# Projections of batches 1 to 3 in pieces beside the attention heads, in an unrolled program

## The reference

```python
Q, K, V = (proj(Wq, bq), proj(Wk, bk), proj(Wv, bv))     # 16 heads of 8 columns
S = jnp.einsum('bhnd,bhmd->bhnm', Q, K) / dh ** 0.5
W_tau = jax.nn.softmax(S, axis=-1)
W_sigma = 1.0 / ((1.0 + jnp.abs(S) / b_) ** 2 + t_ ** 2)
W_sigma = W_sigma / W_sigma.sum(axis=-1, keepdims=True)
f = 0.5 * tau + 0.5 * sigma        # tau = W_tau @ V, sigma = W_sigma @ V
y = f @ Wo.T + bo                  # then a layer norm with ln_w, ln_b, and x is added
```

## Time and profile before

| | us |
|---|---|
| median of 3 runs (2052.15 to 2053.83) | 2053.55 |
| the profiled execution | 2050.47 |
| its span, first to last instruction | 2048.6 |
| first instruction of the heads on VectorE | 97.43 |
| last instruction of the heads | 1611.70 |
| `mix_experts` to the end | the rest |

### The profile page before, as it was taken

How to read it: one execution, slowest core, us unless ns; L and a number is a source line. 1 busy time by engine, 2 the same in 40 slices (tenths; PEclk the granted TensorE clock), 3 DMA queues, 4 the chain that set the end, 5 groups by cost and what they waited for, 6 DMA issues and landing times. The chain is left out here.

```text
span 2048.6 us, 33898 instructions
## 1 busy us (share of the span) xinstructions
PE 1571.4 (77%) x8452; PEld 572.2 (28%) x8579; DVE 1800.0 (88%) x3699; ACT 1634.4 (80%) x1459; POOL 1419.3 (69%) x1070
## 2 busy tenths in 40 slices
PE   4477777877777777777777778777777587788866
PEld 2212222222222222222222222222221243366655
DVE  5799999999999999999999999999998288755556
ACT  3279999999999999999999999999999311222243
POOL 1398999889998899988999899998998112000010
PEclk9689999999999999999999999999999788877878
DMA  3300000000000000000000000000000000000001
GB/s 106 110 4 15 12 12 12 15 14 12 12 12 15 14 12 12 12 15 14 12 12 13 16 12 12 12 13 16 12 12 6 1 1 0 1 0 0 0 1 41
DMA packets 28862, 31.74 MB, mean 15 GB/s; under 512 B 5209, under 2 KB 16544, under 8 KB 28832
## 3 DMA queue, kind: packets, MB, share of 16 engines
q1 hardware_dynamic: 28832, 31.40, 5.0%
HBM read 22.74 MB, written 8.39 MB: 15 GB/s over the span
## 5 line engine op out<-in xcount | busy, mean ns | idle before, releaser
L860 POOL TENSOR_TENSOR sigma_weights<-grown 128x1024 f32<-128x1024 f32 x448 | 845.7, 1894 | 0.0
L718 DVE TENSOR_SCALAR sigma_weights<-ps_sig 128x512 int32<-128x512 int32 x1024 | 693.2, 677 | 26.5 <-PE ps_sig L617 26.5
L604 PE MATMUL ps_acc<-tau_weights,v_operand 128*9 128x512 f32 x2048 | 529.5, 596 | 134.3 <-ACT sigma_weights L779 134.0
L725 DVE TENSOR_TENSOR running_max<-ps_sig,running_max 128x512 f32<-128x512 f32 x896 | 608.2, 679 | 0.0
L833 POOL TENSOR_SCALAR grown<-sigma_weights,shape_operand 128x1024 f32<-128x1024 f32 x448 | 501.7, 1120 | 139.9 <-DVE sigma_weights L718 139.9
L617 PE MATMUL ps_sig<-q_operand,k_operand 96*128 96x512 bf16 x1024 | 400.2, 391 | 180.3 <-DVE running_max L725 165.2
L604 PE MATMUL ps_acc<-sigma_weights,v_operand 128*9 128x512 f32 x2048 | 531.4, 597 | 0.1
L766 ACT ACTIVATE sigma_weights<-sigma_weights,shape_operand 128x2048 f32<-128x2048 f32 x256 | 508.6, 1987 | 11.2 <-POOL sigma_weights L860 11.2
L807 ACT ACTIVATE tau_weights<-ps_tau 128x1024 f32<-128x1024 f32 x512 | 510.8, 998 | 8.0 <-PE ps_tau L635 8.0
L779 ACT ACTIVATE sigma_weights<-sigma_weights 128x2048 f32<-128x2048 f32 x256 | 484.6, 1893 | 0.0
L635 PE MATMUL ps_tau<-q_operand,k_operand 128*128 128x512 bf16 x897 | 277.8, 379 | 7.9 <-DMA q_operand<-max_rows 0.4
(11 more groups left out here) (172 smaller groups left out, 1511.5 us busy)
## 6 DMA issues: line engine op xcount, KB each, us to landing
q_operand<-q_parts SPq DMA_DIRECT2D x192, 48.0 KB
k_operand<-k_parts SPq DMA_DIRECT2D x64, 144.0 KB
q_parts<-parts SPq DMA_DIRECT2D x12, 256.0 KB, 2.9
k_parts<-parts SPq DMA_DIRECT2D x12, 256.0 KB, 2.9
x_res<-in_L_attn_x SPq DMA_DIRECT2D x4, 512.0 KB, 7.0
q_operand<-max_rows SPq DMA_DIRECT2D x128, 2.0 KB
out<-x_res SPq DMA_DIRECT2D x4, 512.0 KB, 3.2
experts<-in_L_ffn_expert_w SPq DMA_DIRECT2D x1, 512.0 KB
```

What stands on the lines that cost most here:

```text
L604: mm = pe.matmul(ps_acc[32 * q:32 * q + COLS, :], vop[:, (slot - 1 + kind) % SLOTS, j, :], weights[:, half * HALF:(half + 1) * HALF], star ...
L718: dve.tensor_scalar(sig[:, tile % SIG_RING, cols].bitcast(I32), ps_sig[:, half, :].bitcast(I32), SIGN_OFF, None, ALU.bitwise_and)\
L725: dve.tensor_tensor(run[:, slot, cols], ps_sig[:, half, :], run[:, slot, cols], ALU.max)\
L860: pool.tensor_tensor(sig[:, tile % SIG_RING, :], t, t, ALU.mult)\
```

## The change

`load_weights`, `project_heads` and `attend_heads` become one block, `attend_heads`, without hardware loops. Its slots are numbered g from 0 to 533 over all heads.

- Before slot 0 only batch 0 is projected. SP loads the x of batches 0 and 1 first; weights and biases are loaded from ScalarE's queue. The x of batches 2 and 3 is loaded after the operands of heads 0 to 2.
- The projections of batches 1, 2 and 3 are pieces, generators that yield the slot at which they are due, from slots 0, 128 and 256 on, each over 21 slots. `Beside.upto` puts a piece between the instructions of its slot. The preparation of the tree's weights and Wo is pieces at slots 24 to 31.
- A batch's q and k are projected in halves of 512 tokens. The two banks `ps_side` are used in turn by all pieces (h0, h1, q0, k0, q1, k1, v0, v1). The buffer `parts` holds one half. ScalarE makes the high part from PSUM and the middle part from `rest`; VectorE makes `rest`; GpSimd makes all low parts. SP stores per half.
- `ps_tau` has one buffer of two banks (its other two became `ps_side`). PE waits with tile g for the exponential of tile g-1.
- Lags: `PV_LAG` 7 to 9, tau 12 to 13. `take_sums` moves with it.
- Both bf16 rows of the row maximum are made by VectorE (ScalarE's L796 is gone).
- GpSimd's copies of v and of the constants are gone: PE and the others read them in place.
- The last step of a head multiplies in PSUM in place and adds from there into `f_tokens`, in the layout that `mix_experts` needs. ScalarE's copy `f_tile` in `mix_experts` (L975) is gone; ln_b is added by GpSimd beside the heads.

The tile that ScalarE squares is the same before and after.

In the diff below, `store_parts` is SP's (due at slots 13 and 19 of a batch's pieces), the first `yield` PE's, the second VectorE's, `high` and `middle` ScalarE's (due at 9, 10, 14.7, 15.5 and at 11, 12, 16.5, 17), the third `yield` GpSimd's.

```diff
-TAU_SHIFT = 4
-PV_LAG = 7
+PV_LAG = 9
+TAU_LAG = 13
+class Beside:
+    def __init__(self, pieces):
+        self.pieces, self.due = pieces, -1.0
+    def upto(self, slot):
+        while self.due <= slot:
+            self.due = next(self.pieces, float("inf"))
...
-        ps_tau = ps("ps_tau", [P, 2, 2, HALF])
+        ps_tau, ps_sig = ps("ps_tau", [P, 2, HALF]), ps("ps_sig", [P, 2, HALF])
+        ps_side = [ps(f"ps_side{i}", [P, HALF]) for i in range(2)]
...
+            def store_parts(b, g):
+                sp.wait_ge(low_ready, 4 * b + 2 * g + 2)
+                for s, scratch in enumerate((q_parts, k_parts)):
+                    for i in range(PARTS):
+                        sp.dma_start(scratch[b * H:(b + 1) * H, i, :, g * HALF:(g + 1) * HALF], parts[:, s, i, :])\
+                            .then_inc(stored, 16)
...
+                for i, (g, s) in enumerate((g, s) for g in range(2) for s in range(2)):
+                    n = u(f"{'qk'[s]}{g}")
+                    yield t0 + 8 + i
+                    read(u(f"h{g}"))
+                    take(n)
+                    done(pe.matmul(bank(n)[:, :], wt[:, s, :], zt[:, g * HALF:(g + 1) * HALF], start=True, stop=True), n)
...
+            def tau_scores(g):
-                        wait(pe, tau_done, g - 1)
+                wait(pe, tau_done, g)
...
+                    yield t0 + (10, 11, 15.5, 16.2)[i]
+                    dve.wait_ge(hi_ready, 4 * b + i + 1)
+                    wait(dve, low_ready, 4 * b + i - 1)
+                    done(dve.scalar_tensor_tensor(out=rest[:, s, :], in0=bank(n)[:, :], scalar=(bq, bk)[s][:, 0:1],
+                                                  in1=parts[:, s, 0, :], op0=ALU.add, op1=ALU.subtract), n)
...
+                def high(i):
+                    g, s = pairs[i]
+                    n = u(f"{'qk'[s]}{g}")
+                    arrived(n)
+                    wait(act, stored, 16 * 2 * PARTS * (2 * b + g))
+                    act.activation(parts[:, s, 0, :], bank(n)[:, :], ACT.Identity, bias=(bq, bk)[s][:, 0:1]).then_inc(hi_ready, 1)
+                def middle(i):
+                    g, s = pairs[i]
+                    read(u(f"{'qk'[s]}{g}"))
+                    act.activation(parts[:, s, 1, :], rest[:, s, :], ACT.Copy).then_inc(mid_ready, 1)
...
+                    yield t0 + (11.5, 12.2, 17, 17.6)[i]
+                    pool.wait_ge(mid_ready, 4 * b + i + 1)
+                    pool.tensor_tensor(parts[:, s, 2, :], rest[:, s, :], parts[:, s, 1, :], ALU.subtract).then_inc(low_ready, 1)
...
+            def complete(of):
+                dve.wait_ge(norm_step, normed(of) + 2)
+                dve.tensor_tensor(result(of - 1), turned[:, :, 0:2, 0:DH], result(of - 1), ALU.add).then_inc(misc_done, 1)
```

More of the change, by code:

```diff
@@ L24 @@
 NH = B * H
+TILES = NH * TB
 HALF = 512
@@ L565, in _, with take, read, done @@
+            beside.upto(ALL)
         @block.tensor
         def _(pe):
-            def turn_running(slot, half, before):
-                wait(pe, misc_done, before)
+            def take(n):
+                wait(pe, side_read[n % 2], n // 2)
+            def read(n):
+                pe.wait_ge(side_read[n % 2], n // 2 + 1)
+            def done(mm, n):
+                mm.then_inc(side_ready[n % 2], 1)
+            def turn_four(n, tile_of):
+                take(n)
+                for t in range(4):
+                    mm = pe.transpose(bank(n)[:, t * P:(t + 1) * P], tile_of(t), ident[:, :])
+                done(mm, n)
@@ new lines, in side, with sigma_scores @@
+            def side():
+                for b in range(B - 1):
+                    yield from project(b + 1, b * BATCH_SLOTS)
+                    if b == 0:
+                        yield from prepare(PREPARE_AT)
+            def sigma_scores(g, half):
+                slot, keys = g // TB % SLOTS, slice(g % TB * P, (g % TB + 1) * P)
+                wait(pe, run_ready, 2 * g - 1 + half)
+                pe.matmul(ps_sig[:, half, :], kop[0:SIGMA_ROWS, slot, keys],
+                          qop[0:SIGMA_ROWS, slot, half * HALF:(half + 1) * HALF], start=True, stop=True).then_inc(sig_ready, 1)
@@ L653, in _ @@
-            stages(pe, stage)
-            turn_sums(NH, misc_before(NH + 1) + 1)
+                        weights = tau[:, (i - TB) % TAU_RING] if kind == 0 else sig[:, i % SIG_RING]
+                        mm = pe.matmul(ps_acc[32 * q:32 * q + COLS, :], v[:, (of - 1 + kind) % (2 * H), j, :],
+                                       weights[:, half * HALF:(half + 1) * HALF], start=j == 0, stop=j == TB - 1)
+                mm.then_inc(pv_done, 1)
+            beside = Beside(side())
+            pe.wait_ge(ident_step, 2)
@@ new lines, in _ @@
+            beside = Beside(side())
+            dve.memset(qop[64:P, :, :], 0.0).then_inc(pads_set, 1)
+            dve.memset(kop[64:P, :, :], 0.0).then_inc(pads_set, 1)
+            dve.wait_ge(pads_set, 2)
+            dve.memset(kop[MROW:MROW + 2, :, :], 1.0).then_inc(pads_set, 1)
+            dve.memset(ps_acc[:, :], 0.0).then_inc(acc_set, 1)
+            pieces = project(0, 0)
+            for _ in range(TB + 1):
+                next(pieces)
+            dve.wait_ge(wt_turned, 1)
+            dve.tensor_copy(wt[:, 0:3, :], ps_tau[:, 0, 0:3 * D].rearrange("p (i d) -> p i d", i=3)).then_inc(wt_ready, 1)
@@ new lines, in normal, with copy_turned @@
+            def normal(z0, b, g):
+                act.wait_ge(shift_ready, z0 + 1)
+                alone(act, act_passed)
+                for t in range(4 * g, 4 * g + 4):
+                    ins = act.activation(h[:, t, :], xt(b, t), ACT.Identity, bias=shift[:, t:t + 1], scale=rstd[:, t:t + 1])
+                ins.then_inc(z_ready, 1)
+            def copy_turned(n, g):
+                arrived(n)
+                done(act.activation(zt[:, g * HALF:(g + 1) * HALF], bank(n)[:, :], ACT.Copy), n)
@@ L1312, in _ @@
         def _(pool):
-            with pool.Fori(0, B) as b:
+            for b in range(B):
                 pool.wait_ge(z_ready, b * TB + TB)
@@ L1320, in _ @@
         def _(pe):
-            with pe.Fori(0, B) as b:
+            for b in range(B):
                 for t in range(TB):
@@ L1550, in _ @@
         def _(sp):
-            with sp.Fori(0, B) as b:
+            for b in range(B):
                 sp.wait_ge(x_done, b * 2 + 2)
```

1116 lines of the change are left out of this document (536 added, 580 removed).

## The result

| us | before | after |
|---|---|---|
| median of 19 runs each | 2051.13 (2049.8 to 2053.83) | 2056.44 (2053.76 to 2062.95) |
| ratio after / before | | 1.0026, 95% interval 1.0019 to 1.0033 |
| the profiled execution | 2050.47 | 2054.09 |
| its span | 2048.6 | 2052.3 |
| first magnitude on VectorE | 97.43 | 45.99 |

The change costs 0.26%, where I had forecast a gain of 0.75%. The time lies in the range of the forecast, on the wrong side of no change. 51 us are won at the start, and all of it, and 4 more, is lost before the span ends. (The forecast started from 2053.55, a median of three runs; over 19 runs the kernel before has 2051.13.)

The account below looks back on a forecast made before the run. ScalarE sets the length of a head (23.2 us), VectorE close behind. The terms -50.4 + 7.0 - 2.7 - 10.1 + 21.9 + 16.8 + 3.2 - 1.1 = -15.4 take 2053.55 to 2038, range 2016 to 2058.

Parts of the forecast that it names:

- The start: Before the heads: VectorE's first magnitude comes at 47 us against 97.4, -50.4, range 42 to 52.
- The ramp: First magnitude to first tau, bound by VectorE: a later tau slot, batch 1's pieces and two waits add +7.0.
- Two are on the path: Beside the pieces: two stalls, the store and the two banks, are on the path, +16.8 together, from 0 to 34.
- Both stops I named: Third high part waits for the store, 4.1 three times; tau waits for two banks, 2.2 for batches 2 and 3.
- The pieces on ScalarE: Behind slot 13: projection pieces and preparation lengthen ScalarE, the bound engine, by +21.9.
- L796: Steady head: this row-maximum instruction leaves ScalarE, 0.16 x 63 = -10.1, if ScalarE stays solid.
- The single `ps_tau` at nothing: In the heads: one tau buffer costs nothing, cover 0.9 us a slot; rival that it bites, 2070, chance 0.14.
- The sign I had promised for "wrong": ScalarE idle before tau in every head, ended by PE: the single buffer, kernel near or above its old time.
- The last step of a head: VectorE's L696 took 1.32 in a head, 0.22 with GpSimd idle; new form priced 0.15, successor near 0.2.
- The middle parts: Beside the heads: casts moved from VectorE to ScalarE put 12 x 0.5 = 6 us on the path.
- The tail and what follows: End of the heads: slower tau tiles and two slots more for PE, +3.2; then `f_tile` leaves the path, -1.1.

Follow-up runs that it names:

- e1: Changed kernel with only the store of the second half moved on SyncE from slot 19 to 22, behind the operand loads: 2045.9, ratio 0.9976.
- e2: Changed kernel with only `parts` holding both halves, so the third high part waits for nothing of its batch: 2034.6, ratio 0.9921.
- e10: e3 with `rest`, middle and low parts of the second half one slot later: 2012.2, ratio 0.9812.
- e5: Changed kernel without the projections of batches 1 to 3 (heads read batch 0's operands and v): 1989.2, ratio 0.9695.
- e7: Changed kernel with the first part of the row maxima (L796) back on ScalarE: 2058.5, ratio 1.0038.
- e6: Kernel before the change with one buffer of tau scores for two, nothing else: 2051.9, ratio 1.0006.
- e9: e3 with `PV_LAG` 8 for 9, the slots of a head's sums and their turning moving too: 2070.7, ratio 1.0094.
- e12: e9 with the turning of a head's sums back in the slot it has with `PV_LAG` 9: 2021.6, ratio 0.9857.
- e8: e3 with the middle-part casts on VectorE right behind `rest`, not on ScalarE: 2026.1, ratio 0.9878.
- e3: Changed kernel with three edits: second-half store behind the operand loads, `parts` for both halves, second-half q and k projections in slots 12 and 13: 2014.3, ratio 0.9825.
- e11: e8 with the middle parts computed on VectorE from PSUM and the high part, not cast from `rest` in SBUF: 2018.6, ratio 0.9842.

## Why the prediction was wrong

The account by stretches of the span, in us. "Last dense tau" is the last tau tile with sigma work beside it (1593.79 + 1.00 before, 1599.48 + 0.92 after, where 0.92 is its pitch; its record of 1.78 ends at 1601.26, and by that end 0.9 moves from the tail to the row above).

| | forecast | measured |
|---|---|---|
| start to the first magnitude | -50.4 | -51.4 |
| ramp, to the first tau | +7.0 | 39.1 - 31.5 = +7.6 |
| first tau to last dense tau | +25.9 | 1515.3 - 1465.9 = +49.4 |
| tail, to the end of the heads | +3.2 | 18.8 - 16.9 = +1.9 |
| what follows | -1.1 | 433.1 - 436.9 = -3.8 |
| sum | -15.4 | +3.7 |

- **The start: right.** 45.99 for 47, but partly by luck. The first half's store had landed at 27.6 for my 29.7, and the second's at 37.6 for 40.4 (landing 1.8 after the last issue, not 2.4); head 0's operand then took 4.7 from its last issue (40.69) to PE's first scores (45.37), where I had 2.4. The two errors nearly cancel. The ramp was right too (7.6 for 7.0).
- **The step that failed: "Two are on the path".** Stops measure 36.6 for 16.8, and this is 19.8 of the 19.1 us that the forecast missed; the others cancel. Both stops I named were there, in the slots named and near their size: 4.9 for 4.1 each, 3.1 for 2.2 each. What was missing:
  - 11.4 us, SyncE's queue. I asked of each queue only whether the moved work fits beside it, not which instruction with a wait stands ahead of which with a due date. The second store waits for GpSimd's low parts; an operand needed three slots later stood behind it. e1 shows it.
  - 4.2 us, VectorE ahead of ScalarE. I let only ScalarE wait for the high part's turn, but `rest` waits for that high part on an engine that is up to a slot ahead, with every magnitude behind it. e2 shows that the store alone doesn't make this stop, e10 that the slot of `rest` does. Its length is about what PE lost at the half clock (2.84 for 1.51 us), a cost that my sum left out; that part is argued, not tested.
- **The pieces on ScalarE: right.** 22.0 by e5 for 20.0 (21.9 less the preparation's 1.9, which e5 keeps).
- **L796: mis-sized.** 0.107 a head for 0.16, and, as it seems, only in undisturbed heads: 4.4 by the spans and 2.0 by the medians, for 10.1. I took a start-to-start distance of one short instruction as its cost; the head's period is the measure. That L796's removal lengthened nothing else stands (e7).
- **The single `ps_tau` at nothing: right** (e6: 0.9 us by the medians, with 0.7 before each of the last tiles; in e10, with the changed order, no stop behind the first tau), but its cover is thin: moving one turn by a slot costs 49 us (e9 against e12). The sign I had promised for "wrong", idle time before tau in every head, is absent in after and present in part in e9.
- **The last step of a head:** 0.212 us in the median, for 0.22.
- **The middle parts.** I priced them as a loss of 6 us against leaving them on VectorE. From first tau to last dense tau, e8 takes 29.8 over e5 and e3 26.1; without their stops of 13.7 and 5.5 that is 16.1 and 20.6, so ten of the casts lie on ScalarE's path with 4.5. But on VectorE they made the kernel 11.8 slower (e8), 4.3 even without waits for GpSimd (e11). In e11 that loss lies before the first tau and behind the heads; beside batches 2 and 3 the two placements came out even (1481.3 and 1481.8). The advice of the Trainium skill that I weighed, Perfetto Trace Analysis, section Optimizing Scalar/DVE Operations, to offload a saturated VectorE to ScalarE, was right here by the times of e3, e8 and e11, but not because ScalarE is free: the gain is the waits for GpSimd (e8 against e11) and the ramp, which VectorE bounds by my account.
- **The tail and what follows.** 1.3 and 2.7 better than forecast. `mix_experts` starts 0.3 after the heads for 2.7 (-2.4, where I had -1.1 for `f_tile`): the table load ahead of `f_tile`, 1.28 us, left the path too. The other 1.4 I haven't traced; these stages are the same in every changed kernel, and in the twelve profiles they took 432.4 (e3) to 435.9 us (e9), 168 to 186 of them at the half clock.
- The medians rose by 5.3 where the spans rose by 3.7; after's runs spread wider (9 us for 4). No experiment explains that.

## What to carry to other kernels

When work is moved beside a solid engine, write out for each in-order queue, DMA queues too, which instruction with a wait now stands ahead of which with a due date; fitting busy times say nothing about that. Here a due slot and the size of a buffer were worth 10.5 and 21.9 us. Place a consumer by the time at which its own engine gets there: one that runs ahead meets a late producer and holds all that is queued behind it.

## What the runs showed of the hardware

- ScalarE's records grow over heads without a stop (tau from 1.02 to 1.79 us in after), with starts 23.04 apart and ends 23.10. From 1236 us on the tau record stays at 1.78 to 1.79, and the starts are 23.10 apart too. They fall back to 1.02 at each stop, and with L796 in every head they never grow. So a start-to-start distance on a solid ScalarE was 0.06 per head too short. Why the ends lag I haven't shown.
- A VectorE cast SBUF to SBUF of 128 x 512 takes 0.41 us with GpSimd idle or in a `grown` (one tensor operand) that began after it, and until 0.3 after the end of a running `tensor_tensor` of GpSimd, at most 2.73. The slower form from PSUM (0.74) was worth 7.5 us.
- TensorE's granted clock was at half (1.2 GHz) in eight stretches of 3.4 to 10.2 us behind the first tau in after, and PE stood still for at least 1.7 us at a time shortly before or during each. PE's float32 matmuls of 512 columns took 1.03 to 1.07 us there for 0.60. So a stop of PE costs twice: at 491.6 the 5.37 us of waiting were followed by 1.3 us of slower work ahead of tau.
